# Attention layer kernel: the exponential of heads 0 and 1 of a key tile as one instruction of 1024 columns or two of 512

## The reference

```
q = rope(xn @ Wq); k = rope(xn @ Wk); v = xn @ Wv       # 16 heads of 64 for q; k and v have 512 columns
k, v = each column repeated twice                       # so 32 different columns per head
scores = softmax(q @ k * scale)                         # per batch and head, 1024 x 1024
out = x + (scores @ v) @ Wo + ffn(xn)                   # ffn: silu(gate) * up, hidden size 384
```

## Time and profile before

| | |
|---|---|
| median of 3 runs | 1211.19 us (1210.43 to 1213.35) |
| the profiled execution's own time | 1210.01 us |
| span of the profile, first to last instruction | 1208.2 us |
| TensorE matmul (PE) busy | 1161.2 us, 96% |
| TensorE weight loads (PEld) busy | 642.0 us, 53% |
| VectorE (DVE) | 892.1 us, 74% |
| ScalarE (ACT) | 697.7 us, 58% |
| GpSimd (POOL) | 878.2 us, 73% |
| granted TensorE clock, mean | 0.989 of full speed |

### The profile page before, as it was taken

One profiled execution on the slowest core, in us unless ns is written; L12 is line 12 of the kernel. 1 busy time (PEld: TensorE's weight loads), 2 busy tenths in 40 slices (PEclk: granted clock), 3 DMA queues, 4 the chain that ended last, 5 costly groups with the idle time before them and its releaser, 6 DMA issues.

```text
span 1208.2 us, 19402 instructions
## 1 busy us (share of the span) xinstructions
PE 1161.2 (96%) x6288; PEld 642.0 (53%) x6288; DVE 892.1 (74%) x1009; ACT 697.7 (58%) x1074; POOL 878.2 (73%) x274
## 2 busy tenths in 40 slices
PE   5898999999999999999999999999999999999985
PEld 4786455555555555555555555555555555554432
DVE  7685778777777778777777777777777777876622
ACT  3333556666666656666666656666666556665563
POOL 2312777887778877787777887787777887787775
PEclk9898999999999999999999999999999999999997
DMA  6652707062421517062422517061422517050000
GB/s 222 172 238 99 213 2 217 1 188 65 142 76 62 156 36 215 0 197 55 141 75 74 143 36 215 0 202 49 148 68 87 131 36 215 0 125 1 4 1 17
DMA packets 56287, 124.58 MB, mean 103 GB/s; under 512 B 7968, under 2 KB 19488, under 8 KB 54048
## 3 DMA queue, kind: packets, MB, share of 16 engines
q1 hardware_dynamic: 56224, 123.89, 35.0%
HBM read 53.08 MB, written 10.49 MB: 53 GB/s over the span
## 4 chain that ended last, share of the span: by engine, by line
PE 90%; DVE 3%; POOL 2%; ACT 1%; issue 1%; DMA 1%; SPq 1%; POOLq 0%; ACTq 0%; DVEq 0%
PE bank_s L542 24%; PE scores L379 22%; PE bank_o L394 20%; PE scores L362 7%; PE bank_m L370 3%; PE bank_m L404 3%; PE bank_m L430 2%; PE bank_m L407 2%; POOL prob_sum L1018 2%; PE scores L480 2%; PE bank_s L497 1%; PE bank_m L414 1%; PE bank_m L421 1%; DVE prob L917 1%; DMA x_all<-x 1%
## 5 line engine op out<-in xcount | busy, mean ns | idle before, releaser
L824 DVE TENSOR_REDUCE row_max<-scores 128x1 f32<-128x1024 f32 x512 | 605.7, 1217 | 194.7 <-PE scores L379 194.7
L1018 POOL TENSOR_TENSOR prob_sum<-prob_sum,prob 128x2048 f32<-128x2048 f32 x128 | 586.3, 4581 | 112.9 <-DVE prob L917 103.8
L542 PE MATMUL bank_s<-qk_pack 98*128 98x512 f32 x1024 | 383.6, 432 | 12.8 <-ACT prob L768 6.7
L779 ACT ACTIVATE prob<-bank_s 128x512 f32<-128x512 f32 x512 | 285.1, 596 | 172.3 <-PE bank_s L542 165.1
L768 ACT ACTIVATE prob<-bank_s 128x1024 f32<-128x1024 f32 x256 | 262.5, 1025 | 187.8 <-PE bank_s L542 180.5
L379 PE MATMUL scores<-qk_pack 96*128 96x512 f32 x1024 | 340.5, 419 | 1.1 <-DVE row_max L824 1.1
L542 PEld LDWEIGHTS bank_s<-qk_pack 98*128 98x128 f32 x1024 | 183.0, 189 | 232.4 <-ACT prob L768 144.3
L394 PE MATMUL bank_o<-prob,v 128*32 128x512 f32 x2048 | 273.6, 606 | 0.9 <-ACT prob L779 0.9
L379 PEld LDWEIGHTS scores<-qk_pack 96*128 96x128 f32 x1024 | 177.0, 190 | 136.8 <-DVE row_max L824 109.1
L963 POOL TENSOR_TENSOR qk_stage<-rope,qk_stage 128x512 fp32r<-128x512 f32 x64 | 82.1, 1283 | 90.8 <-ACT qk_stage L653 90.8
L1011 POOL TENSOR_TENSOR prob_sum<-prob 128x2048 f32<-128x2048 f32 x32 | 146.4, 4575 | 0.0
(11 more groups left out here) (88 smaller groups left out, 679.5 us busy)
## 6 DMA issues: line engine op xcount, KB each, us to landing
qk_pack<-qk_stage SPq DMA_DIRECT2D x384, 128.0 KB, 3.5
table<-tables SPq DMA_DIRECT2D x16, 2048.0 KB, 9.9
w_stage<-w_scratch SPq DMA_DIRECT2D x14, 640.0 KB, 4.7
v<-v_stage SPq DMA_DIRECT2D x32, 256.0 KB, 3.2
xT_scratch<-xT_hl SPq DMA_DIRECT2D x4, 1024.0 KB, 9.5
x_stage<-xT_scratch SPq DMA_DIRECT2D x4, 1024.0 KB, 5.4
w_scratch<-w_split SPq DMA_DIRECT2D x1, 2560.0 KB, 15.1
x_all<-x SPq DMA_DIRECT2D x4, 512.0 KB, 12.5
```

The costliest lines, as they stand in the source:

```text
L542: mm(bank_s[:, h % 2, :], qk_pack[j][0:SCORE_K, 1, kt // QT, h, (kt % QT) * 128:(kt % QT + 1) * 128], qk_pack[j][0:SCORE_K, 0, t, h, :], s ...
L779: A(prob[:, kt % RING, h, :], bank_s[:, h % 2, :], ACT.Exp).then_inc(prob_ready, 1)
L824: V.tensor_reduce(row_max[:, m:m + 1], scores[:, at:at + 2, :].rearrange("p c k -> p (c k)"), axis=AX.X, op=ALU.max).then_inc(max_read, 1)
L1018: TT(prob_sum[:, t], prob_sum[:, t], prob[:, kt % RING], ALU.add).then_inc(sum_done, 1)
```

## The change

The wide exponential becomes a loop over heads 0 and 1, each of 512 columns, each with its own wait for the score and its own count on `prob_ready`. A key tile now counts 4 (`NE = HG`, and HG is 4), `EXP_OF` goes, and the wait of a score becomes one formula: heads 0 and 1 give NE times the key tiles before minus 1 and minus 0, as before the exponentials of heads 2 and 3 of the last key tile; heads 2 and 3 give plus 1 and plus 2. All other waits on `prob_ready` are multiples of NE and mean the same key tiles.

```
-NE = 3
-
-EXP_OF = [0, 0, 1, 2]
+NE = HG
...
                 def score(kt, h):
-                    at_least(pe, prob_ready, NE * (KT * u + kt) + (EXP_OF[h - 2] + 1 if h > 1 else EXP_OF[h + 2] + 1 - NE))
+                    at_least(pe, prob_ready, NE * (KT * u + kt) + h - 1)
...
-                    act.wait_ge(score_ready, 32 * u + 4 * kt + 2)
-                    A(prob[:, kt % RING, 0:2, :], bank_s[:], ACT.Exp).then_inc(prob_ready, 1)
+                    for h in (0, 1):
+                        act.wait_ge(score_ready, 32 * u + 4 * kt + h + 1)
+                        A(prob[:, kt % RING, h, :], bank_s[:, h, :], ACT.Exp).then_inc(prob_ready, 1)
```

## The result

| | before | after |
|---|---|---|
| median, both in the same session | 1211.77 us (20 runs, 1209.72 to 1213.35) | 1213.51 us (20 runs, 1211.88 to 1215.28) |
| ratio of the runs, 95% interval | 1 | 1.0020 (1.0014 to 1.0025) |
| the profiled execution: own time, span | 1210.01, 1208.2 us | 1212.06, 1210.0 us |
| ScalarE busy | 697.7 us | 709.5 us |
| granted TensorE clock, mean | 0.989 | 0.989 |

The kernel became slower by 1.7 us at the median, 2.4 us by the ratio. That is less than the 0.3% that I called no change, but it is resolved, and I had forecast 1.3 us less.

A forecast was written before the change was run, and what follows sets the result against it. TensorE's matmuls were taken as the bound (90% of the span). Gains of 0.4 + 0.28 + 0.6 = 1.3 us took the median from 1211.19 to 1209.9 us, called "no change"; range 1206.3 to 1214.0.

The forecast's parts named there:

- What that gives in the middle (28 units): Middle units: no gain or loss, since the product with v stands between in PE's order; value 0.
- The start of unit 0: Unit 0, where PE waits 2.02 us: head 2's score starts 0.68 us earlier; gain 0.4 us (bounds 0 and 0.7).
- The clock rival: Start of unit 0: shorter PE idling keeps the clock up, 4.1 us less in all, 1207.1 us; chance 17%.
- Units 29 and 30: First key tile of each: head 2's exponential starts earlier, 0.14 us gained a unit, 0.28 us for both.
- Unit 31: Last unit, before y_part: earlier halves and a true weight-load wait removed in key tiles 0 to 2; gain 0.6 us.
- The second release costs: Every key tile: PE pays 0.05 us more for head 3's own release, 13 us slower, 1223 to 1224; chance 7%.
- The listed wait is real: Scores' weight loads: 163 idle places truly wait for the exponential, 69 us less, 1142 us; 3% with a smaller variant.
- The change does nothing: Both ends: gains lost on POOL and VectorE, 1211.2 us; chance 73% together with the forecast.

The follow-up runs named there:

- e2: Kernel before, wide exponential throughout, with already-met waits added so that ScalarE's loop starts at 315 instead of 283; 1214.39 us, ratio 1.0026 to the kernel before.
- e1: Changed kernel plus 15 already-met wait instructions, so that ScalarE's loop starts at 330 instead of 315; 1209.16 us, ratio 0.9993 to the kernel before.
- e9: Kernel before, wide exponential, with 19 pairs of already-met waits added so that ScalarE's loop starts at 321; 1211.29 us, ratio 0.9997 to the kernel before.
- e4: Kernel before with the split only in units 0 to 3 and 28 to 31, wide loop starting at 315; 1212.62 us, ratio 1.0017 to the kernel before.
- e10: Kernel before with the split only in units 0 to 3 and 28 to 31, waits added, wide loop starting at 330; 1209.91 us, ratio 0.9988.
- e5: Kernel before, wide exponential, with 18 pairs of already-met waits added so that ScalarE's loop starts at 319; 1224.77 us, ratio 1.0101 to the kernel before.
- e7: Kernel before with the split in unit 0 alone, wide loop starting at 291; 1211.07 us, ratio 0.9987 to the kernel before.
- e3: Kernel before with the split only in the loop (units 4 to 27), loop starting at 283; 1210.90 us, ratio 1.0004 to the kernel before.
- e8: Kernel before with the split in units 28 to 31 alone, wide loop starting at 283; 1212.20 us, ratio 0.9996 to the kernel before.

## Why the prediction was wrong, and where it was right

**The step that failed** is "What that gives in the middle (28 units)... Value 0". Its argument is borne out for every key tile but five: PE in the middle is as full as before, the halves are hidden, and the weight loads stand where they stood. What it left out is that an added instruction has a place as well as a duration. 32 instructions ahead of the loop moved its start from 283 to 315, six instructions ahead of the end of a block, and the five returns to it cost 0.67 + 0.72 + 0.73 + 0.67 + 0.68 = 3.5 us (of the 3.75 in that part). e2 shows it without the change, and e1 shows the change without it. The trace before already held the first half of the mechanism, and I didn't look there: at each back edge 2.4 to 2.6 us pass from ScalarE's branch to its next instruction. The row of the exponential behind it doesn't tell, since its 1.92 us of idle time are mostly a wait for the scores (1.66 in e9, where nothing is fetched).

The Trainium skill (Runtime: NRT & Kernel Launch, Instruction fetch mechanics) has the rule that I didn't weigh: a taken branch to a target outside the part of the program at hand makes the engine wait for a DMA of the target's page. The trace agrees, with 383.14 - 380.73 = 2.4 us from the branch to the next instruction. Of the crossing from one block to the next the Trainium skill says in the same section that it is "mostly hidden"; right behind a branch it isn't, as 385.19 - 383.14 = 2.05 us show, and the five crossings cost 3.5 us. The blocks of the Trainium skill are 16 KiB of 256 instructions; ScalarE's transfers here are of 8192 bytes, one every 128 instructions.

**The start of unit 0** was sized 0.4 and gave 0.4 to 0.65. The rows answer to the earlier trace rows:
```profile
111.27 0.70 PE L540 MATMUL bank_s<-qk_pack 98*128 98x512 f32 x2 [0.90 <-DMA qk_pack<-max_rows]
...
111.84 1.28 ACT L767 ACT_TABLE_LOAD   x1 [0.84 <-PE bank_s L540]
...
113.13 1.08 ACT L767 ACTIVATE prob<-bank_s 128x512 f32<-128x512 f32 x2
...
113.78 0.98 PE L540 MATMUL bank_s<-qk_pack 98*128 98x512 f32 x2 [1.36 <-ACT prob L767]
```
From the first score to head 2's it is 113.78 - 111.27 = 2.51 us, before 3.17: 0.66 earlier, where I had 0.68. What was left of it at the copy of the maxima depends on the clock. In e1, e4 and e10, whose low clock is as long as before, it is 0.56 to 0.65 us (30.61 to 30.70 against 31.26; other kernels that are wide in unit 0 take 30.98 to 31.29 there). Against e5, which is wide and has the same short low clock as the changed kernel, it is 29.83 - 29.42 = 0.41 us.

What comes before the first score (+0.57) has no exponential in it, and lies between 110.2 and 111.7 us in the twelve profiled executions, whatever the kernel.

**The clock rival** came about by half in the profiled execution. The low clock lasts 3.4 us there, not 6.8, and the rest of the -1.84, 1.2 to 1.4 us, is from that:
```profile
110.50:114.60 4.10, 1.97 (x6) 1.16 (x7) 1.23 (x1) 3.14 (x5) 3.38 (x2) 1.00 0.18 65
114.60:118.10 3.50, 3.50 (x14) 1.82 (x13) 2.36 (x2) 1.98 (x5) 1.41 (x1) 0.51 0.56 170
118.10:121.50 3.40, 3.03 (x18) 1.73 (x10) 2.11 (x2) 2.01 (x4) 1.48 (x2) 1.00 0.65 170
```
But the split doesn't decide it. e1, e4 and e10 have the split and 6.8 us; e7 has it and 3.4; e5 has the wide exponential and 3.4. So the 1.2 to 1.4 us are luck of the profiled execution. Whether the split makes the short stretch more likely, one trace of each kernel can't say.

**Units 29 and 30** gained 0.30 and 0.32 us instead of 0.14, unit 28 0.12. The 0.14 of ScalarE's order is in it. The rest, about 0.17, is on VectorE: the cast of the maxima, ahead of the next unit's scores, takes 0.52 us where the exponentials are wide and 0.33 where they are split. Before, then after:
```profile
1151.65 0.52 DVE L830 CAST max_hl<-row_max 128x16 fp32r<-128x16 f32 x1
```
```profile
1153.54 0.33 DVE L829 CAST max_hl<-row_max 128x16 fp32r<-128x16 f32 x1
```
In e3, whose last units are wide, it takes 0.52 to 0.54 us there and 0.33 to 0.37 in its split loop; in e8, whose last units are split, 0.35 to 0.37 there and 0.52 to 0.53 in its wide loop. So it goes with the exponential beside it. Why is open, and that the 0.17 us of the unit are this cast was only argued from the sizes.

**Unit 31** was sized 0.6 and gave 0.74. From the copy of `bank_o` to `y_part` it is 1168.60 - 1162.59 = 6.01 us, before 6.75, and the true wait of the weight load is gone as forecast: 0.84, before 1.11.
```profile
1162.59 0.59 ACT L726 COPY o_raw<-bank_o 128x512 f32<-128x512 f32 x1
...
1168.60 0.59 ACT L743 COPY y_part<-bank_m 128x512 f32<-128x512 f32 x1
```
```profile
1179.12 0.30 PEld L540 LDWEIGHTS bank_s<-qk_pack 98*128 98x128 f32 x2 [0.84 <-ACT prob L767]
```
POOL's sums, two in 9.26 us, set the rest, as forecast. The last part is 0.75 us longer, which the split doesn't explain either: it is 41.4 us in ten of the twelve profiled executions, of wide and split kernels alike, and 40.6 to 40.7 in those of before and of e3, where the low clock of the tail begins and ends elsewhere.

**The other rivals.** "The second release costs" is refuted: 256 key tiles have a release more, and yet 27 units of e1 and e3 take 915.0 and 914.6 us against 914.8, which is 0.01 us a unit either way. "The listed wait is real" is refuted by the 139 places that are still there. "The change does nothing" is refuted at the ends, and what the split is worth without the block end (e1 and e10: 0.8 and 1.5 us less by the ratios) fits the 1.3 us that I had. The single terms aren't resolved by times: e7, with the split in unit 0 alone, came out 1.6 us less (0.5 to 2.7), where my term was 0.4. With the missing term of 3.5 us the sum would have been +2.2 us, against 1.7 to 2.4 measured.

Two numbers of the prediction were wrong without weight for the outcome. The price of "the listed wait is real" takes the 0.25 us off twice (it is already in the 0.35); the gain per place would be up to 0.68 us, and the time some 1100 us. And 0.3% was too coarse a bound for "no change": with 20 runs of each kernel the ratio was known to 0.06%.

## What to carry to other kernels

Where an engine's instructions are changed ahead of a loop or in it, count where the loop's first instruction lies in that engine's own stream, and look at the first work after a back edge for a stop that waits for nobody (the chain's "issue", or a releaser that is long done). A few waits that are already met, put ahead of the loop, move its start; on this kernel that was worth more than the change. Judge a change by the same cut of the unrolled and the looped part, since one of its sides can hide the other.

## What the runs showed of the hardware

- ScalarE's instructions come in blocks that end at fixed places of its stream: here ahead of number 321, where it stops, and by the times of the transfers also ahead of 449, 577 and 705. After a branch back to a block that has to be fetched, its next instruction came 2.4 to 2.7 us after the branch, and the next block 2.0 to 2.4 us after that. With 14 or more instructions of the loop in the first block this is hidden here, with 6 it costs 0.5 to 1.0 us, and with 2 it costs 1.5 to 1.7 us, and 3.2 to 3.4 where the clock falls behind it.
- A loop of 331 instructions that lay in three of these blocks (e9, e10) was not fetched again: 0.24 to 0.26 us from the branch to the next instruction, and no transfer. The same loop across four blocks was fetched in every iteration.
- The clock's low stretches differ from execution to execution, in wide and split kernels alike: at unit 0 they are 3.4 or 6.8 us long, and at the start of unit 31 there was none (six of the twelve, e8 among them), 3.4 us (e1, e4, e10) or 6.8 us (e2, e5, e7). The part from `bank_o` to `y_part` then takes 6.0 to 6.7, 7.4 to 7.6 or 8.8 to 8.9 us. Two windows of PE at the start of unit 31, e8 and then e7, with the columns of the earlier trace rows:
```profile
1160.00:1166.00 6.00, 5.51 (x32) 2.63 (x32) 0.00 (x0) 4.71 (x10) 3.18 (x1) 1.00 0.00 0
```
```profile
1160.10:1166.80 6.70, 6.44 (x20) 3.23 (x21) 0.00 (x0) 3.61 (x6) 3.50 (x1) 0.50 0.00 0
```
  It is a large part of the 3 to 5 us by which the runs of one kernel differ. e8's runs fall in two groups of times with nothing between, and their mean granted clock parts them in the same way (0.988 against 0.985 to 0.986). In which place the low stretch of such a run lies, only a trace would show.
- A cast of 128 x 16 numbers on VectorE took 0.52 us or 0.33 us, depending on whether ScalarE's exponentials beside it were of 1024 or of 512 columns.
